# A graph network kernel on one core: the second normalisation in five chunks, with the prologue, the fillers, two readers and the casts changed

## The reference

```python
h = relu(layernorm(x))                               # first normalisation
# L0: two hypergraph convolutions over (src = node, dst = hyperedge)
conv(x, W, b): e = B_inv * segment_sum((x @ W)[src], dst)
               return D_inv * segment_sum(e[dst], src) + b
x = x + conv(relu(conv(h, W1, b1)), W2, b2)
h = relu(layernorm(x))                               # second normalisation
# L1: edge network
e = silu(silu([h[src], h[dst], w] @ eW1 + eb1) @ eW2 + eb2)
agg = segment_sum(e, src)
x = x + silu([h, agg] @ nW1 + nb1) @ nW2 + nb2
```

## Time and profile before

| | us |
|---|---|
| three runs | 8148.05, 8153.98, 8159.79 |
| their median | 8153.98 |
| the profiled execution | 8149.92 |
| its span, first to last instruction | 8148.2 |

### The profile page before, as it was taken

One profiled execution on the slowest core, in us unless ns is written; L12 is line 12 of the kernel. 1 busy time (PEld: TensorE's weight loads), 2 busy tenths in 40 slices (PEclk: granted clock), 3 DMA queues, 4 the chain that ended last, 5 costly groups with the idle time before them and its releaser, 6 DMA issues. The chain is left out here.

```text
span 8148.2 us, 251180 instructions
## 1 busy us (share of the span) xinstructions
PE 7491.0 (92%) x79908; PEld 7026.0 (86%) x79908; DVE 7075.0 (87%) x15335; ACT 5267.2 (65%) x12972; POOL 3200.4 (39%) x4180
## 2 busy tenths in 40 slices
PE   4899999999999998999888899949999999999998
PEld 3788888888888887999888899938999999999997
DVE  6999999999999995888888888868899999999996
ACT  2888998989898981000477788835666666666664
POOL 1999999999999990000000000001111111111110
PEclk9999999999999999999999999969999999999999
DMA  2677777777777778666799899964333334333434
GB/s 69 138 165 175 167 176 165 176 167 173 169 174 169 172 172 201 191 190 190 199 222 221 207 244 241 241 175 121 114 114 114 113 115 116 115 113 115 116 114 101
DMA packets 1533191, 1309.72 MB, mean 161 GB/s; under 512 B 810544, under 2 KB 1347556, under 8 KB 1531404
## 3 DMA queue, kind: packets, MB, share of 16 engines
q1 hardware_dynamic: 1515918, 1269.86, 63.7%
q0 software_dynamic: 14112, 26.84, 1.2%
q10 hardware_dynamic: 2240, 0.66, 0.1%
HBM read 778.02 MB, written 361.62 MB: 140 GB/s over the span
## 5 line engine op out<-in xcount | busy, mean ns | idle before, releaser
L719 POOL TENSOR_SCALAR OH<-iot,kd 128x102 bf16<-128x102 bf16 x3440 | 2659.4, 793 | 0.0
L2329 POOL DMA_INDIRECT Qx<-tab_q,tidx x294 | 349.1, 1188 | 4511.3 <-DVE skt L2363 2390.3
L1573 ACT ACTIVATE AF<-RG 128x1536 fp32r<-128x1536 uint8 x686 | 1022.8, 1491 | 1192.6 <-DMA RG<-adj 889.9
L1024 ACT ACTIVATE RB<-PS 128x512 uint8<-128x512 f32 x2401 | 1409.7, 601 | 90.7 <-PE PS L884 46.0
L1543 PE MATMUL wp<-AF,XS 128*128 128x256 f32 x9604 | 1215.7, 284 | 143.4 <-issue 84.6
L900 PE MATMUL HP<-T3a,RB 128*128 128x193 bf16 x9604 | 1209.0, 249 | 119.1 <-ACT RB L1024 114.5
L1543 PEld LDWEIGHTS wp<-AF,XS 128*128 128x128 f32 x9604 | 1158.1, 191 | 176.9 <-issue 174.4
L2350 ACT ACTIVATE Z<-Zb 128x512 f32<-128x512 f32 x882 | 556.1, 630 | 978.4 <-DVE Zb L2407 978.2
L900 PEld LDWEIGHTS HP<-T3a,RB 128*128 128x128 fp8e4 x9604 | 864.7, 98 | 203.7 <-issue 149.6
L1639 DVE CAST AF<-RG 128x2048 fp32r<-128x2048 uint8 x686 | 817.5, 1223 | 151.2 <-DMA RG<-adjT 74.8
L2300 PEld LDWEIGHTS p<-eW2s,Y 128*128 128x128 f32 x7056 | 923.2, 191 | 24.0
(11 more groups left out here) (344 smaller groups left out, 14691.2 us busy)
## 6 DMA issues: line engine op xcount, KB each, us to landing
RG<-adjT SPq DMA_DIRECT2D x1372, 224.0 KB, 7.6
sdb<-bk SPq DMA_DIRECT2D x245, 768.0 KB
adj<-RB SPq DMA_DIRECT2D x343, 448.0 KB, 2.9
adjT<-RT SPq DMA_DIRECT2D x686, 224.0 KB, 3.8
RG<-adj SPq DMA_DIRECT2D x686, 224.0 KB, 4.5
sdb<-bk SPq DMA_DIRECT2D x49, 384.0 KB
WR<-wk SPq DMA_DIRECT2D x882, 9.0 KB
tab_p<-Pst SPq DMA_DIRECT2D x25, 512.0 KB, 3.0
```

Source lines behind the costliest of these rows:

```text
L719: ins = e.tensor_scalar(OH[:, g * GT + k, :], iot1[:, 0:KEYS], kd[:, g * GT + k:g * GT + k + 1], None, ALU.is_equal)
L1024: e.activation(RB[n % NSLOT][:, k, :].bitcast(u8).rearrange("p (n x) -> p n x", x=2), bank(u)[:, :].rearrange("p (x n) -> p n x", x=2), AC ...
L1573: e.activation(floats((b + n) % 3, VB, PB), counts(n, VB, PB), ACT.Copy).then_inc(h_ca, 1)
```

## The change

1. Prologue: the clip goes out of `norm.vector` (`clip=False`), and ACT's copy of the transposed group takes a Relu in its place. Two transposes of 128 x 128 turn two blocks each, and two matmuls multiply them with `Wd`, a 128 x 128 tile with W1 twice on its diagonal. That takes two more loads of W1 on ACT's queue and two small memsets on DVE. `SPACE1` is 92 and stands ahead of PE's waits.
2. Counting stage: ACT's `record` waits for the records in `S` (`p_s`), not for DVE's copy of the keys; DVE's `filled` waits for `record` (`a_w`).
3. First wide hop: in pieces 1 and 4 of a turn DVE casts 6 tiles and ACT 8 (`vectors(n)`).
4. The 114 marks of `SPACE2` go.
5. Second normalisation: five chunks of five groups. Chunk 0 runs ahead; those after it run on DVE between the residuals of the groups, with squares and roots on ACT. `tab_n` is stored in five parts. The clip goes here too, into ACT's copies of the transposed `hT2` and, in the final network, `hT`.

```diff
-SPACE1 = 136
-SPACE2 = 114
+SPACE1 = 92
...
-                link(e.tensor_scalar(to, to, 0.0, None, ALU.max))
+                if clip:
+                    link(e.tensor_scalar(to, to, 0.0, None, ALU.max))
...
+            loads.append((Wd[n * F:(n + 1) * F, n * F:(n + 1) * F], W1))
...
-                            e.activation(lin.hT[g % 2][:, :, :].rearrange("p j n -> p (j n)"), lin.pt[g % 2][0:F, :], ACT.Copy).then_inc(lin.copied, 1)
+                            e.activation(hTw[g % 2][:, :, :].rearrange("p j n -> p (j n)"), ptw[g % 2][:, 0:2 * P], ACT.Relu).then_inc(lin.copied, 1)
...
-                    e.wait_ge(norm.steps, 8)
+                    spaced(e, SPACE1)
+                    e.wait_ge(norm.steps, 7)
                     e.wait_ge(s_w, 16 * len(loads))
                     e.wait_ge(s_fill, 3)
-                    lin.tensor(e, 0, X0, nW["W1s"])
-                    spaced(e, SPACE1)
+                    for g in range(NG + 1):
...
+                            for y in range(2):
+                                ins = e.transpose(ptw[g % 2][:, y * P:(y + 1) * P],
+                                                  X0[:, g * GB + 2 * y:g * GB + 2 * y + 2, :].rearrange("p j f -> p (j f)"), idn[:, :])
...
+                            for y in range(2):
+                                ins = e.matmul(pow_[q % 2][:, y * P:(y + 1) * P], lhsT=hTw[q % 2][:, y, :], rhs=Wd[:, :], start=True, stop=True)
...
                         def record(c):
 
-                            e.wait_ge(v_f, c * NVF + 1)
+                            e.wait_ge(p_s, c * NGR + NGR)
+                            past(e, v_f, c * NVF)
...
                             past(e, p_tr, i)
+                            e.wait_ge(a_w, i * NAW + 3)
                             e.tensor_copy(vi[0:K, :], S[0:K, 0:P]).then_inc(v_f, 1)
...
+                        def vectors(n):
+
+                            return VB - 2 if r == 1 and n in (1, 4) else VB
...
-                                        e.tensor_copy(floats((b + n) % 3, 0, VB), counts(n, 0, VB)).then_inc(h_cd, 1)
+                                        e.tensor_copy(floats((b + n) % 3, 0, vectors(n)), counts(n, 0, vectors(n))).then_inc(h_cd, 1)
...
-                    spaced(e, SPACE2)
...
-                    e.wait_ge(norm2.steps, 8)
                     for g in range(NG + 1):
                         if g < NG:
+                            if g % CG == 0:
+                                e.wait_ge(norm2.steps, 6 * (g // CG + 1))
...
+                            m, r = divmod(q, CG)
+                            if r == 1 and m + 1 < NC:
+                                squares(m + 1)
+                            if r == 2 and m + 1 < NC:
+                                roots(m + 1)
...
-                    norm2.vector(e, X, acc64, H1n[:, :, :])
...
+                    def centred(m):
+
+                        mean, to = of_chunk(sm["m"], m), of_chunk(H1n, m)
+                        link(m, 1, e.tensor_reduce(mean, of_chunk(X, m), AX, ALU.add))
+                        link(m, 2, e.tensor_scalar(mean, mean, 1.0 / F, None, ALU.mult))
+                        link(m, 3, e.tensor_tensor(to, of_chunk(X, m), mean.unsqueeze(2).to_broadcast([P, CB, F]), ALU.subtract))
...
+                        m, r = divmod(g, CG)
+                        if m + 1 < NC:
+                            if r == 0:
+                                centred(m + 1)
+                            elif r == 1:
+                                spread(m + 1)
+                            elif r == 2:
+                                scaled_rows(m + 1)
```

More of the change, by code:

```diff
@@ L198, in __init__, with vector @@
                 self.steps, self.root, self.n = sem(f"n_{name}"), sem(f"r_{name}"), 0
[L200 removed]
+            def vector(self, e, X, sq, to=None, clip=True):
                 to = Hn if to is None else to
@@ L241, in gnn_kernel @@
         W22 = sbt(root, "W22", [P, F], fp32)
+        Wd = sbt(root, "Wd", [P, 2 * F], fp32)
         Wab = sbt(root, "Wab", [P, 2 * HID], fp32)
@@ L362, in gnn_kernel @@
             rs = [sbt(st, f"rs{n}", [P, GB, F], fp32) for n in range(2)]
-            lin.buffers(st, "w")
+            ptw, pow_ = ([pst(st, f"{n}w{k}") for k in range(2)] for n in ("pt", "po"))
+            hTw = [sbt(st, f"hTw{k}", [P, 2, P], fp32) for k in range(2)]
             calls[0] += 1
@@ L2006, in _ @@
                 def _(e):
-                    e.wait_ge(norm2.steps, 8)
-                    e.dma_start(tab_n.rearrange("(b p) f -> p b f", p=P), H1n[:, :, :]).then_inc(u_q, 16)
                     for g in range(NG):
+                        if g % CG == 0:
+                            m = g // CG
+                            e.wait_ge(norm2.steps, 6 * (m + 1))
+                            e.dma_start(of_chunk(tab_n.rearrange("(b p) f -> p b f", p=P), m), of_chunk(H1n, m)).then_inc(u_q, 16)
                         e.wait_ge(u_2, g + 1)
@@ L2042, in _, with squares, roots @@
                 def _(e):
-                    norm2.scalar(e)
+                    def squares(m):
+                        e.wait_ge(norm2.steps, 6 * m + 3)
+                        e.activation(sqd[:, :, :], of_chunk(H1n, m), ACT.Square).then_inc(norm2.root, 1)
+                    def roots(m):
+                        e.wait_ge(norm2.steps, 6 * m + 4)
+                        e.activation(of_chunk(sm["m"], m), of_chunk(sm["v"], m), ACT.Sqrt, bias=eps[:, 0:1], scale=1.0 / F).then_inc(norm2.root, 1)
+                    squares(0)
+                    roots(0)
                     for g in range(NG + 2):
@@ L2048, in _ @@
                                 e.wait_ge(u_m, u_b + g - 1)
-                            e.activation(hT2[g % 2][:, :, :].rearrange("p j n -> p (j n)"), pt2[g % 2][:, 0:2 * P], ACT.Copy).then_inc(u_c, 1)
+                            e.activation(hT2[g % 2][:, :, :].rearrange("p j n -> p (j n)"), pt2[g % 2][:, 0:2 * P], ACT.Relu).then_inc(u_c, 1)
                         if g >= 1 and g <= NG:
@@ L2063, in _, with link, spread, scaled_rows @@
                 def _(e):
-                    norm2.vector(e, X, acc64, H1n[:, :, :])
+                    def link(m, n, ins):
+                        ins.then_inc(norm2.steps, 1)
+                        e.wait_ge(norm2.steps, 6 * m + n)
+                    def centred(m):
[3 more added lines that the diff above has]
+                        link(m, 3, e.tensor_tensor(to, of_chunk(X, m), mean.unsqueeze(2).to_broadcast([P, CB, F]), ALU.subtract))
+                    def spread(m):
+                        e.wait_ge(norm2.root, 2 * m + 1)
+                        link(m, 4, e.tensor_reduce(of_chunk(sm["v"], m), sqd[:, :, :], AX, ALU.add))
+                    def scaled_rows(m):
+                        var, to = of_chunk(sm["v"], m), of_chunk(H1n, m)
+                        e.wait_ge(norm2.root, 2 * m + 2)
+                        link(m, 5, e.reciprocal(var, of_chunk(sm["m"], m)))
+                        link(m, 6, e.tensor_tensor(to, to, var.unsqueeze(2).to_broadcast([P, CB, F]), ALU.mult))
+                    centred(0)
+                    spread(0)
+                    scaled_rows(0)
                     for g in range(NG + 1):
@@ L2656, in _ @@
                                 e.wait_ge(f_u, g - 1)
-                            e.activation(hT[g % 2][:, :], ph[:, 0:256], ACT.Copy).then_inc(f_hc, 1)
+                            e.activation(hT[g % 2][:, :], ph[:, 0:256], ACT.Relu).then_inc(f_hc, 1)
                         if g >= 1:
```

30 lines of the change are left out of this document (24 added, 6 removed).

## The result

| | before | with the change |
|---|---|---|
| median | 8149.25 (5 runs, 8138.01 to 8159.79) | 8092.59 (5 runs, 8079.85 to 8119.78) |
| profiled execution | 8149.92, span 8148.2 | 8079.85, span 8078.0 |

The ratio of the runs is 0.994, with a 95% interval from 0.9919 to 0.996: the change saves 33 to 66 us. The profiled pair is 70 us apart. The forecast was 8072, its range 8005 to 8125.

The account below looks back on a forecast made before the run. Each stage was given its own limit: PE in the prologue's tail, POOL in counting, DVE mostly in the wide hop, stores in the tables. Terms -34 + 0 - 16 + 0 - 20 - 8 = -78 took 8149.92 to 8072, range 8005 to 8125.

Parts of the forecast that it names:

- Prologue: Start of the kernel: clip off the chain, shorter waits, wide products and hidden marks save 34 us (28 to 38).
- 11.2 + 3.5: Prologue: last nine groups every 1.65 us instead of 2.9, -11.2; first product wait and smaller ones shorter, -3.5.
- Rival E: Prologue: Relu or wide products are not cheaper, marks alone give -15.5, result 8091; chance counted within the likeliest case's 0.64.
- Counting stage: Counting loop: POOL is the bound and waits for neither engine, so the handshake only moves waits; 0, kept within ±25 us.
- A: Counting loop was held by the handshake after all; 134.2 us of waits partly or wholly come out, 7938 to 8035; chance 0.13.
- C: Counting stage: POOL's one-hots slow down beside DVE's moved work, 30 to 50 ns more each giving 8175 to 8244; chance 0.05.
- Casts: First wide hop: DVE's smaller casts save 0.27 us each, two a turn in 33 turns; -16 us, bounds -8 to -18.
- Rival B: Wide hop and tables: transfers hide both DVE gains, from casts and normalisation chunks; 8095 to 8115, chance 0.14.
- Marks ahead of the extra transposes: Before the second normalisation: removing these marks gives 0, since DVE's add waits for the read of x, not PE.
- Second normalisation: Chunking cuts the head by 31.2 us; later chunks lose 9 and the pipeline refill some 2, so -20.
- Edge stage: Edge loop, unedited: moved PE code shortens instruction waits at the jumps; 0 to -14 us, taken -8.
- Rival D: Edge loop: a jump back misses its code, up to +133 us over 23 jumps, giving 8213; chance 0.04.

Follow-up runs that it names:

- run 7: Changed kernel with the prologue's narrow transposes (128x64) and products (64x64) as before; first one-hot at 157.9 us against 140.3, timed once, no ratio.
- run 9: Changed kernel with its 92 marks behind the prologue's last product instead of in front; first one-hot at 153.7 us against 140.3, no ratio.
- run 4: Changed kernel with the counting stage's handshake as before, record waiting for DVE's key copy; counting loop 2851.5 us against 2846.3, ratio 0.9967 to the kernel before.
- run 1: Changed kernel with DVE casting eight tiles in every piece again; first wide hop 719.9 us, median 8066.25, ratio 0.9915 to the kernel before.
- run 5: Changed kernel with DVE's six-tile cast walked with the byte of the pair outermost; first wide hop 705.1 us, ratio 0.9874 to the kernel before.
- 6: Changed kernel with the whole second normalisation ahead of the tables, tab_n still in five stores; head 35.9, tables 120.0 us, ratio 0.9973 to the kernel before.
- 10: Changed kernel with the whole second normalisation ahead of the tables and tab_n in one store; head 35.9, tables 114.5 us, timed once, no ratio.
- run 8: Changed kernel with 290 marks instead of 92 at PE's start; edge stage 2528.1 us against 2508.6, ratio 0.9936 to the kernel before.
- 2: Changed kernel with DVE casting four tiles and ACT ten in pieces 1 and 4; first wide hop 690.5 us, median 8043.51, ratio 0.9894 to the kernel before.
- 3: Changed kernel with DVE's six tiles cast as two instructions, four and two; first wide hop 707.4 us, ratio 0.9913 to the kernel before.
- 11: Changed kernel with four tiles on DVE in pieces 1 and 4, and 136 marks ahead of PE's waits; median 8023.63, ratio 0.9849 to the kernel before.
- 12: Changed kernel with 136 marks and four-tile DVE casts in pieces 1, 3, 5 of search turns, 3 of the third; median 8010.22, ratio 0.9833 to before.

## Why the prediction held, and where it did not

The time lay in the range and on the side that was forecast; it was 21 us above the 8072 that I gave, against a forecast gain of 78. That it came so near is partly luck: one term was wrong by 50 us, and what made up for it was not in the forecast, 29 us of it in a stage without an edit.

*Prologue.* Right: -37.2 for -34. The 17.9 of the wide products are run 7's, the 0.13 of a mark run 9's; the clip's 3.5 is its length in the earlier trace rows, and no run brings it back. The products gave more than the 11.2 + 3.5 that I gave them, since the tail's groups came every 0.9 to 1.3 us and not 1.65. ("A quarter of the matrix passes" is a slip: the products' rows fall from x8 to x4 a group, by half, and the sum uses the half.) Rival E, products that are no cheaper, is refuted by run 7.

*Counting stage.* Right in its reason: POOL busy all the time, its one-hots unmoved, waits that only change names. It was given 0 and gave 4.3 in the loop, which run 4 brings back, and 5.5 in the tail, which it does not. Rivals A and C, either way, did not come. (In C, 793 less 555 is 238 ns and not 228, which changes nothing in it.)

*Casts.* Wrong, the one step that failed. "Two tiles 0.27 by the quarter" took a time in proportion to the elements, from one shape. DVE's cast of the new shape wasn't in the trace of before, and my bounds, -8 to -18, left no room for a dearer one. Measured: +0.53 us a cast instead of -0.27, +34.4 us instead of -16; run 1 takes exactly that away, and run 5 shows that the count of three outermost is the cause. The Trainium skill, "Advanced Engine Details and Errata", under 2x-2p requirements, states when DVE takes two elements a cycle from two ports: both operands in SBUF, and the outermost dimension that is not one even in source and destination, or odd and equal in both. The source's is 3 here, and the destination's one run of 1536. By that rule the cast goes at half the pace, and 1.75 against 0.96 us agrees. With the measured +34 in place of -16 the sum is -28 and the time 8122; what brought the profiled execution back to 8080 are the parts that I put too low, some 13 us in the prologue, the counting stage and its tail, and the 29 of the second wide hop. The median, 8093, has no trace, so how it is made up is not shown. Rival B, casts that give nothing because the loads bound the hop, did not come either: the casts lost for their own reason, and the share of the loads fell.

*Marks ahead of the extra transposes.* No run tells them apart; that stretch is 39.5 before and 38.7 after.

*Second normalisation.* Right: head -31.4 for -31.2; tables +10.2 for +11. The reason was half right. Chunks took 19.1 us, not 17.7. By runs 6 and 10 the chunks cost the tables 5.5 us, and the five stores, which I had given nothing, another 5.5; so the 11 that I gave the chunks was twice too much, and that the sum came out is luck.

*Edge stage.* Right in size, -7.8 for -8. That the place of the code sets the jumps is shown (run 8, with nothing but marks changed). The Trainium skill, "Runtime: NRT & Kernel Launch", instruction fetch mechanics, says that a jump outside the window stalls; the estimate of -12 that the prediction draws from it is near the 11.7 that the 22 jumps lost, and the 2.85 of the new wait behind the loop was not foreseen. But the same counting failed in run 8, which should have brought back jumps of 1.45 us and brought 1.96, so the rule gives a direction here and no size. Rival D, jumps that become dearer, did not come.

*What is left.* The second wide hop has the same code in all runs and took 618.6 to 651.1 us. It seems to be held by its loads, DMA share 1.05 and 1.04:

```profile
4754.20:5311.10 556.90, 522.38 (x4370) 510.83 (x4369) 460.55 (x519) 449.94 (x336) 0.00 (x0) 0.99 1.05 242
```

```profile
4744.10:5273.00 528.90, 507.24 (x4370) 502.39 (x4369) 456.45 (x518) 448.08 (x337) 0.00 (x0) 1.00 1.04 254
```

The first is before, the second after: the same 4370 products at 242 and at 254 GB/s. Each kernel has one trace, so the spread could be the kernel's or the execution's. The times speak for the execution: of the kernels that were timed several times, the five whose traces have the hop at 618.6 to 625.0 us (after, 1, 2, 3, 5) have a profiled execution 13 to 26 us under their own median, and in the six with 630.5 to 651.1 (before, 4, 6, 8, 11, 12) it is 0 to 7 above. It would also explain why the profiled pair is 70 us apart and the medians 57. Whether the kernel before can reach 622 was not seen in a second trace of it, and what sets the rate stays open.

## What to carry to other kernels

Before work is moved from one engine to another in smaller or larger pieces, look at the counts of the access pattern, not only at their product: here three instead of four outermost made a cast of fewer elements cost 43% more. A piece of three can be walked in another order, or cut to an even one. Where one engine is busy for 99% of a stage, waits of over a hundred microseconds on the others may be worth four or five; read the bound first. Filler instructions belong ahead of a wait, where they are hidden. A shift of code by 198 instructions made a stage of 2509 us 19.5 longer, so the place of a loop is to be measured with each edit.

## What was not expected of the hardware

- VectorE, uint8 to fp32, 128 partitions: 421 ns for 512 elements, 689 for 1024, 956 for 1536 and 1221 for 2048 with an even outermost count; 1747 for 1536 with three. ScalarE's time does not show that: 1485, 1916 and 2345 ns for 1536, 2048 and 2560, with 3, 4 and 5 outermost.
- A jump back on TensorE took 0.43 to 1.96 us on average in these kernels, and 1.96 instead of 0.92 when 198 marks at the program's start were all that changed (run 8); the edge stage, 23 iterations of 102 us, took from 2499 (run 7) to 2528 us (run 8).
- A semaphore increment on TensorE's stream costs 0.13 us (12.4 / 92, run 9).
- One stage at a DMA share of 1.04 to 1.05 ran at 242 or at 254 GB/s with the same code.
